# State-space powers from a table of exponents on TensorE and ScalarE sines; phases of the chunk states on VectorE

## The reference

```
dt   = exp(log_dt);  A = -exp(A_re_log) + 1j * A_im;  dtA = A * dt
C    = (C_re + 1j * C_im) * expm1(dtA) / A
K    = 2 * einsum('hn,hnl->hl', C, exp(dtA[:, :, None] * l)).real      # l = 0 .. L-1
y    = causal_convolution(z, K) + z * D_skip                           # z = layernorm(h)
y    = gelu(y);  out = W @ y + b;  h = h + out[:H] * sigmoid(out[H:])   # four such layers
```

## Time and profile before

| | |
|---|---|
| median of 3 executions | 1387.14 us (1383.18 to 1394.52) |
| profiled execution, own time | 1394.2 us |
| its span (first to last instruction) | 1392.4 us |
| mean granted TensorE clock | 0.817 of full |
| busy: PE, DVE, ACT, POOL | 939.7, 936.1, 482.8, 508.0 us |
| state-space stage (four layers and prologue) | 0 to about 464 us of the span |

### The profile page before, as it was taken

How to read it: one execution, slowest core, us unless ns; L and a number is a source line. 1 busy time by engine, 2 the same in 40 slices (tenths; PEclk the granted TensorE clock), 3 DMA queues, 4 the chain that set the end, 5 groups by cost and what they waited for, 6 DMA issues and landing times.

```text
span 1392.4 us, 19437 instructions
## 1 busy us (share of the span) xinstructions
PE 939.7 (67%) x7176; PEld 625.3 (45%) x7176; DVE 936.1 (67%) x1586; ACT 482.8 (35%) x1204; POOL 508.0 (36%) x384
## 2 busy tenths in 40 slices
PE   4052262262273617999999967759889788979877
PEld 4032042141042306787878743324466443546543
DVE  5999899799785663464645468968855346955443
ACT  3133043043031422121212141016677334768622
POOL 4862832832710360000000032437934133954310
PEclk9575685685685758999999978979989779979968
DMA  1151071071071418454544040000011200012100
GB/s 59 40 92 32 3 130 32 2 129 30 0 129 30 183 44 146 91 91 90 90 90 90 0 147 0 0 0 0 16 46 49 80 24 25 1 31 62 32 0 30
DMA packets 60445, 75.52 MB, mean 54 GB/s; under 512 B 37544, under 2 KB 42036, under 8 KB 58676
## 3 DMA queue, kind: packets, MB, share of 16 engines
q1 hardware_dynamic: 60376, 74.60, 24.5%
HBM read 52.11 MB, written 1.51 MB: 39 GB/s over the span
## 4 chain that ended last, share of the span: by engine, by line
PE 39%; DVE 29%; POOL 13%; issue 10%; ACT 5%; DMA 2%; SPq 0%; DVEq 0%; POOLq 0%; ACTq 0%
PE bank L960 6%; PE bank L962 6%; PE bank L961 6%; POOL rest L1190 3%; ACT rest L1143 3%; POOL rest L1180 3%; PE bank L1378 2%; POOL rest L1186 2%; PE bank L641 2%; DVE kept L379 2%; DVE main L534 2%; PE bank L1387 2%; DVE rest L453 2%; PE bank L1445 2%; PE bank L1446 2%
## 5 line engine op out<-in xcount | busy, mean ns | idle before, releaser
L406 POOL TENSOR_TENSOR kept<-kept 128x8 f32<-128x8 f32 x20 | 4.0, 201 | 456.9 <-DVE kept L383 456.9
L1143 ACT ACTIVATE rest<-bank,main 128x128 f32<-128x128 f32 x256 | 113.4, 479 | 12.4 <-POOL main L1201 10.8
L641 PE MATMUL bank<-main,rest 128*128 128x512 f32 x64 | 38.6, 759 | 92.3 <-DVE main L573 86.5
L807 ACT ACTIVATE x_high<-main 128x512 fp32r<-128x512 f32 x48 | 30.3, 633 | 199.1 <-DVE main L881 199.1
L960 PE MATMUL bank<-x_high,w_low 128*128 128x512 f32 x192 | 76.7, 399 | 20.4 <-DVE x_low L886 20.4
L629 PE MATMUL bank<-main 128*32 128x64 f32 x1024 | 22.4, 270 | 99.2 <-DMA main<-main 98.8
L1209 POOL TENSOR_TENSOR rest<-rest,main 128x512 f32<-128x512 f32 x64 | 65.4, 1043 | 47.3 <-DVE main L1274 47.3
L420 ACT ACTIVATE main<-bank,kept 128x128 f32<-128x128 f32 x40 | 14.5, 469 | 185.7 <-POOL kept L413 185.7
L881 DVE TENSOR_TENSOR main<-kept,rest 128x512 f32<-128x512 f32 x48 | 33.0, 690 | 68.1 <-PE bank L962 43.7
L961 PE MATMUL bank<-x_low,w_high 128*128 128x512 f32 x192 | 76.2, 397 | 0.0
L960 PE MATMUL bank<-hid_high,w_low 128*128 128x512 f32 x192 | 75.6, 394 | 0.7 <-DVE main L905 0.7
(11 more groups left out here) (283 smaller groups left out, 2873.1 us busy)
## 6 DMA issues: line engine op xcount, KB each, us to landing
rest<-share_d SPq DMA_DIRECT2D x4, 3072.0 KB, 21.4
rest<-share_d SPq DMA_DIRECT2D x4, 2304.0 KB, 20.3
main<-main SPq DMA_DIRECT2D x32, 256.0 KB, 5.1
main<-k_pad SPq DMA_DIRECT2D x16, 512.0 KB, 7.4
rest<-main SPq DMA_DIRECT2D x32, 256.0 KB, 3.4
main<-w_dram SPq DMA_DIRECT2D x2, 3072.0 KB, 14.5
main<-main SPq DMA_DIRECT2D x32, 128.0 KB, 2.3
rest<-tables_dram SPq DMA_DIRECT2D x2, 2048.0 KB, 9.2
```

The lines of the kernel that those rows point to most:

```text
L641: last = T.matmul(bank[4 + 2 * (b % 2) + k][:, :], w_out[:, k * P:(k + 1) * P], rhs, start=True, stop=True)
L1143: last = A.activation(probs[:, p, 4 * r + m, :], bank[2 * p + r][:, m * P:(m + 1) * P], ACT.Exp, scale=row_scale[:, c, r, m:m + 1], bias=r ...
```

## The change

- The angles and exponents no longer come from broadcast products of GpSimd and VectorE. `dta` (rate and angle per turn, 64 columns) is transposed on TensorE, copied by ScalarE to `dtaT`, and multiplied with a table `expo` (64 rows of 3072 floats, block-diagonal, loaded once: 768 KB) in PSUM: 4 products of 512 columns for the near angles, 2 for the far ones, 4 for the magnitudes' exponents. All have 32 rows of contraction.
- ScalarE adds `MAGIC` to round to whole turns (`s4_act_round_near`, `_far`), VectorE subtracts in one instruction each (`s4_dve_near_turns`, 2048 wide, `s4_dve_far_turns`, 1024 wide), in place of three parts and a clamp. ScalarE takes the sines at all 64 near powers directly (three passes of 2048) and exponentiates the magnitudes in PSUM (one pass of 2048).
- `pow_re`, `pow_im` are two VectorE instructions of 2048 with the magnitude read from PSUM. There are no anchors, `k_re`, `k_im`, and no GpSimd part.
- The coefficients go into the weights (`sel_re`, `sel_im`, 128x4 per channel) and the kernel rows come from 64 products of 64 columns (each with weights of its own), laid on four partition groups; ScalarE copies them with 4 + 4 copies, and SyncE writes them with 4 DMAs instead of 1.
- `g_re`, `g_im` (the phases times the coefficient) move from GpSimd to the end of `s4_dve_powers`, six VectorE instructions of 1024. GpSimd keeps `decay`, which waits for the layer's `s4_u_re`.
- The prologue makes layer 0's angles ahead of `LN_A` on VectorE. The loops over layers are written out; marker increments (`turn`) are gone; some semaphores of later stages are merged.

The diff, cut to its core:

```diff
-        def s4_dve_angles(dve, G):
...
-            V.tensor_tensor(mag, dta[:, 0, :].unsqueeze(2).to_broadcast([P, HG, NEAR]),
-                            expo[:, 0:NEAR].unsqueeze(1).to_broadcast([P, HG, NEAR]), ALU.mult).then_inc(sem("s4_marg"), 1)
-        def s4_dve_reduce(dve, chain, G):
...
-            for part in (TWO_PI_1, TWO_PI_2, TWO_PI_3):
-                link(V.scalar_tensor_tensor(theta, turns, -part, theta, ALU.mult, ALU.add))
-            V.tensor_scalar(theta, theta, 3.1415925, -3.1415925, ALU.min, ALU.max).then_inc(sem("s4_theta"), 1)
+        def s4_dve_near_turns(dve, G):
+            dve.wait_ge(sem("s4_rounded"), G * 2 + 1)
+            nc.vector.scalar_tensor_tensor(turns, turns, MAGIC, near(HIGH_BANKS), ALU.subtract, ALU.subtract).then_inc(sem("s4_turns"), 1)
...
+        def s4_dve_powers(dve, chain, G, mag):
+            V.tensor_copy(s0, pow_re[:, :, FIRST])
+            link(V.tensor_copy(mag1, mag[:, :, FIRST]))
+            V.tensor_tensor(pow_im, pow_im, mag, ALU.mult).then_inc(sem("s4_pow_im"), 1)
+            V.scalar_tensor_tensor(pow_re, pow_re, 1.0, mag, ALU.subtract, ALU.mult, reverse0=True).then_inc(sem("s4_pow_re"), 1)
...
-            V.tensor_tensor(four(pow_re), hi(anc_re), lo(anc_re), ALU.mult)
-            link(V.tensor_tensor(four(k_re), hi(anc_im), lo(anc_im), ALU.mult))
-            V.tensor_tensor(pow_re, pow_re, k_re, ALU.subtract).then_inc(sem("s4_pow_re"), 1)
-            dve.wait_ge(sem("s4_pow_re"), G + 1)
-
-            V.tensor_tensor(k_re, pow_re, c2_re.unsqueeze(2).to_broadcast([P, HG, CHUNK]), ALU.mult).then_inc(sem("s4_k_re"), 1)
+            V.tensor_tensor(sel_re, sel[:, 0, :].unsqueeze(1).to_broadcast(wide), c2_re.unsqueeze(2).to_broadcast(wide), ALU.mult)
+            V.tensor_tensor(sel_im, sel[:, 1, :].unsqueeze(1).to_broadcast(wide), c2_im.unsqueeze(2).to_broadcast(wide), ALU.mult).then_inc(sem("s4_sel"), 1)
...
+            V.tensor_tensor(gr, phi_c, c2r, ALU.mult)
+            V.tensor_tensor(gi, phi_c, c2i, ALU.mult)
+            V.tensor_tensor(g_x, phi_s, c2i, ALU.mult)
+            link(V.tensor_tensor(g_y, phi_s, c2r, ALU.mult))
+            V.tensor_tensor(gr, gr, g_x, ALU.subtract)
+            V.tensor_tensor(gi, gi, g_y, ALU.add).then_inc(sem("s4_phases"), 1)
...
+        def s4_pe_near_angles(pe, G):
+            pe.wait_ge(sem("s4_dtaT"), G + 1)
+            for k in range(4):
+                last = nc.tensor.matmul(bank[4 + k][:, :], dtaT[HG:2 * HG], expo[HG:2 * HG, 512 * k:512 * k + 512], start=True, stop=True)
+            last.then_inc(sem("s4_x_ps"), 1)
...
+            pe.wait_ge(sem("s4_sel"), L + 1)
+            for hh in range(HG):
+                q, at = hh // PIECE, CHUNK * (hh % PIECE)
+                dst = bank[4][32 * q:32 * q + GROUPS, at:at + CHUNK]
+                T.matmul(dst, sel_re[:, hh, :], pow_re[:, hh, :], start=True, stop=False)
+                last = T.matmul(dst, sel_im[:, hh, :], pow_im[:, hh, :], start=False, stop=True)
+            last.then_inc(sem("s4_k_ps"), 1)
...
             pe.wait_ge(sem("s4_back"), (L + 1) * (HG // 2))
-            pe.sem_inc(sem("turn"), 1)
+            if more:
+                s4_pe_near_angles(pe, L + 1)
             pe.wait_ge(sem("s4_z"), L + 1)
...
+            if more:
+                s4_pe_far_angles(pe, L + 1)
+                pe.wait_ge(sem("s4_in"), L + 1)
+                s4_pe_exponents(pe, L + 1, 0)
...
+        def s4_act_sines_near(act, G):
+            act.wait_ge(sem("s4_turns"), G * 2 + 1)
+            if G:
+                act.wait_ge(sem("s4_pow_moved"), G * 128)
+            A.activation(pow_im, turns, ACT.Sin, scale=-TURN)
+            A.activation(pow_re, turns, ACT.Sin, scale=-TURN / 2).then_inc(sem("s4_sin"), 1)
+            act.wait_ge(sem("s4_sin"), G * 2 + 1)
+            A.activation(pow_re, pow_re, ACT.Square, scale=math.sqrt(2.0)).then_inc(sem("s4_sin"), 1)
...
             if more:
-
-                act.wait_ge(sem("s4_phases"), L + 1)
-                s4_act_decay(act, L + 1)
-            if more:
-                s4_act_sines(act, L + 1, CLOSE, "s4_sin")
-
+                s4_act_round_near(act, L + 1)
+                s4_act_sines_near(act, L + 1)
+                s4_act_round_far(act, L + 1)
+                s4_act_sines_far(act, L + 1)
+                s4_act_magnitudes(act, L + 1, LOW_BANKS)
             act.wait_ge(sem("s4_u"), L + 1)
-            if more:
-                s4_act_sines(act, L + 1, FAR, "s4_sin_far")
...
+        def s4_pool_phases(pool, chain, G):
+            pool.wait_ge(sem("s4_mag"), G * 2 + 1)
+            if G:
+                pool.wait_ge(sem("s4_u_re"), G)
+            G_.tensor_tensor(decay[:, :, 1:CHUNKS], r_chunk[G % 2].unsqueeze(2).to_broadcast([P, HG, CHUNKS - 1]),
+                             ones.unsqueeze(1).to_broadcast([P, HG, CHUNKS - 1]), ALU.mult).then_inc(sem("s4_decay"), 1)
```

More of the change, by code:

```diff
@@ L81, in exponents @@
 def exponents():
-    e = [LOW - 1 - b for b in range(LOW)] + [LOW * (HIGH - 1 - a) for a in range(HIGH)] + [CHUNK * c for c in range(CHUNKS)]
-    return np.array(e, np.float32)
+    near, far = CHUNK - 1 - np.arange(CHUNK), CHUNK * np.arange(CHUNKS)
+    rows = [np.kron(np.eye(HG), e) for e in (near, far)]
+    return np.tile(np.concatenate(rows, axis=1), (2, 1)).astype(np.float32).reshape(-1)
 class Chain:
@@ new lines, in s4_pe_far_angles, with s4_pe_exponents @@
+        def s4_pe_far_angles(pe, G):
+            pe.wait_ge(sem("s4_turns"), G * 2 + 1)
+            for k in range(2):
+                at = NEAR_COLS + 512 * k
+                last = nc.tensor.matmul(bank[4 + k][:, :], dtaT[HG:2 * HG], expo[HG:2 * HG, at:at + 512], start=True, stop=True)
+            last.then_inc(sem("s4_x_ps"), 1)
+        def s4_pe_exponents(pe, G, first):
+            for k in range(4):
+                last = nc.tensor.matmul(bank[first + k][:, :], dtaT[0:HG], expo[0:HG, 512 * k:512 * k + 512], start=True, stop=True)
+            last.then_inc(sem("s4_x_ps"), 1)
@@ new lines, in s4_act_rates, with s4_act_dtaT, s4_act_round_near @@
+            A.activation(r_chunk[G % 2], dta[:, 0, :], ACT.Exp, scale=float(CHUNK)).then_inc(sem("s4_mag"), 1)
+        def s4_act_dtaT(act, G):
+            act.wait_ge(sem("s4_dtaT_ps"), G + 1)
+            nc.scalar.activation(dtaT, bank[6][0:2 * HG, 0:P], ACT.Copy).then_inc(sem("s4_dtaT"), 1)
+        def s4_act_round_near(act, G):
+            act.wait_ge(sem("s4_x_ps"), G * 3 + 1)
+            if G >= 1:
+                act.wait_ge(sem("s4_phases"), G)
+            nc.scalar.activation(turns, near(HIGH_BANKS), ACT.Copy, bias=MAGIC).then_inc(sem("s4_rounded"), 1)
@@ L725, in s4_pool_angles @@
-        def s4_pool_angles(pool, chain, G):
-            G_ = nc.gpsimd
-            wide = [P, HG, N_EXP]
-            def link(instruction):
-                chain.link(instruction)
-                pool.sem_inc(sem("turn"), 1)
-            pool.wait_ge(sem("s4_dta"), G + 1)
-            link(G_.tensor_tensor(theta, dta[:, 1, :].unsqueeze(2).to_broadcast(wide),
-                                  expo.unsqueeze(1).to_broadcast(wide), ALU.mult))
-            link(G_.tensor_scalar(turns, theta, 1.0 / (2 * math.pi), MAGIC, ALU.mult, ALU.add))
-            G_.tensor_scalar(turns, turns, MAGIC, None, ALU.subtract).then_inc(sem("s4_turns"), 1)
```

358 lines of the change are left out of this document (169 added, 189 removed).

## The result

The changed kernel takes **1336.8 us** (median of 4 executions, 1330.3 to 1343.5) against 1386.3 for the kernel before (4 executions): a ratio of 0.963, interval 0.957 to 0.970. It is faster by 50 us, and the forecast of 1320 had expected 67.5. The profiled execution took 1339.3, its span is 1337.5.

The account below looks back on a forecast made before the run. VectorE, held up by GpSimd's work, was taken to bound the state-space layers. Savings of 28.4 (prologue, layer 0), 35.6 (two middle layers) and 3.5 (layer 3) sum to 67.5: 1387.1 becomes 1319.6, said as 1320, range 1304 to 1350.

Parts of the forecast that it names:

- rival D: VectorE's holds come from something other than GpSimd and stay: minus 20 instead of minus 67, 1367 us; chance 0.04.
- rival C: Weight load and product do not overlap in the kernel rows, 0.22 us a record: +80, so 1400 us; chance 0.05.
- the wait: VectorE idle in a middle layer from the norm's end at 20.0 to ScalarE's rounding of near angles at 25.3.
- The chain: TensorE and ScalarE work before the near turns: kernel rows, copies, near angles, rounding; done 25.3 us into a middle layer.
- rival A: The new TensorE and ScalarE chain is off the path, VectorE alone sets the time: 1312 us; chance 0.14.
- the pace of the state products: State products behind the near angles in middle layers run at 2.4 GHz: 3.6 us instead of 7.05.
- Rival B: TensorE at 1.2 GHz from kernel rows through state products: +11 each middle layer, 1359 us; chance 0.10 with half-way cases.
- the lower end of the range: Fastest total time the forecast allowed: 1304 us, with the new chain off the path and a lighter prologue.
- The 6.9 us for the kernel rows: Lower estimate for a layer's 128 kernel-row records, by columns from L641 at 0.054 each; the forecast took 7.5.
- The term costed at nothing: Written-out layer loops and markers costed at 0, since layer 0 was written out already and its L619 took no longer.
- Layer 0: Prologue and first layer: prologue powers end at 68.9, the layer at 149.9 against 178.3, minus 28.4 us.
- The second half of the change: The six phase instructions moved from GpSimd to VectorE's powers, costed at 6.9 us of the 17.3 us powers.

Follow-up runs that it names:

- e9: Changed kernel with the kernel-row products and ScalarE's copies of layers 1 to 3 moved into the layer before: 1331.9 us, 0.957 of the kernel before.
- e2: Changed kernel with each layer's Toeplitz transfer issued only after its state products: 1335.9 us, 0.958 of the kernel before.
- e7: Changed kernel with angle and exponent products reading 64 rows instead of 32, the added rows zero: 1341.0 us in one execution.
- e6: Kernel before the change with only the six phase instructions moved from GpSimd to the end of VectorE's powers: 1406.4 us, ratio 1.011.
- e4: Changed kernel with the six phase instructions given back to GpSimd, behind decay: 1325.9 us, 0.951 of the kernel before.
- e3: Changed kernel with one unused product added behind each group of four back transposes: 1353.4 us, 0.973 of the kernel before.

## Why the prediction was right, and where it was not

**Right in kind.** The blocking went (rival D): L529 2.50 for four, small instructions 0.2, powers 16.7 against 17.3. Load and product overlap in the kernel rows (rival C): 0.056 a record, where 0.058 was taken and 0.19 would have turned the sign. The norm was done at 20.0, as forecast to a tenth; near angles at 22.8 (23.2), near turns at 27.0 (27.6), the wait at 4.72 and 5.41 (5.3). The chain is on the path, as e9 shows by taking it off, so rival A fell. The Trainium skill (TensorE: Matmul & The Clock Gate, Back-to-back issue gap) would have had 81 ns a record; by the 0.056 of this trace the rule does not hold for these products, whose weights are 4 columns wide.

**The step that failed** is the pace of the state products: "The pause before them falls away, so I take 2.4 GHz: 3.6 instead of 7.05". The pause ahead of them did fall away. The clock fell all the same, within or right behind the near angles, and with the stop inside them they take 8.5 us in layer 1. This moved the last transpose from 30.1 to 32.1 there, and to 33.0 in layer 2, where the transposes of the powers were slow too; the powers, 0.6 shorter, and small savings gave 1.1 of it back. The state products end 4.5 us later than forecast in layer 1 and only 2.0 of it shows, as the transposes wait for the near turns anyway. The small savings that gave part of it back were in no term of the forecast: luck. The forecast read the granted clock as a matter of gaps alone. The runs show that the rows of the products ahead matter: with 32 of the 128 the clock falls, with 64 it stays for the state products. Rival B named this clock, but began it at the kernel rows, which ran at 1.00; it was right for the state products alone.

Two slips in the working touch the lower end of the range only. The 6.9 us for the kernel rows "by columns alone" is not what L641's row gives: 3.70 us for eight records of 512 columns is 0.058 for 64, or 7.4 us. And rows between 6.9 and 18 move a layer by minus 0.6 to plus 10, not from minus 2.

**The term costed at nothing** is "The written-out loops and the markers I cost at 0". Layer 0 had been written out before and had no pause, but its program was shorter and its state products came at the pace of 1.2 GHz. With the written-out program the products of layer 3, which did run at 2.4 GHz, stop for 3.85, and with the clock lost in that pause they take 9.25 instead of 3.6. That is 5.7 of the 6.1 by which layer 3 missed. e2 takes back 3.4 of it.

**Layer 0** was 3.7 late. The prologue's powers end at 70.9 instead of 68.9, and the last transpose at 98.5 instead of 93.8: 2.0 from the prologue, 0.7 from near turns that come later still, 2.0 from the pace of the state products, and 1.0 is made good behind them. In the prologue TensorE's far angles and exponents, kernel after, ran at half pace from end to end, and VectorE waited for TensorE's next work behind them:

```profile
26.81 3.77 PE L604 MATMUL psum<-main 32*128 32x512 f32 x4 [4.37 <-DVE rest L444]
...
32.96 7.19 PE L610 MATMUL psum<-main 32*128 32x512 f32 x8 [2.37 <-DVE rest L450]
...
41.23 1.66 DVE L393 TENSOR_SCALAR kept<-psum,kept 128x512 f32<-128x512 f32 x2 [1.29 <-PE psum L366]
```

The forecast had some 2 us for the far angles and nothing on the path for the exponents. The half pace here is not a matter of 32 rows alone: e7 had it with 64.

**The second half of the change** was costed rightly, 6.9 on VectorE's path, and counted as part of a net gain. e6 and e4 show that it should have been judged by itself: once the powers need no GpSimd, GpSimd can make the phases during the transposition and the gate, where VectorE has nothing with two SBUF inputs to be held.

## What to carry to other kernels

When an engine held by another is freed, ask again for every job that was moved to get away from the hold: the phases were better left on GpSimd, in a stretch where VectorE only transposes or waits. Cost a stretch of small products by the clock that its neighbours leave, and look at how many rows the products ahead use, not only at gaps. Faster work that is fed by a written-out program can run into its own instruction supply: look for pauses marked "issue" with nothing that releases them, and at what the DMA queues moved in the microseconds before, ahead of counting a saving.

## What the runs showed of the hardware that was not expected

- The granted clock fell to 0.50 in a stretch where TensorE was 100% busy with 32-row products of 512 float32 columns. With 64 rows and the same columns it stayed at 1.00 through the near angles and 152 records and more behind them. Where it was low already, in the prologue, eight records took 7.19 us with 32 rows and with 64, while the kernel rows there (128 rows, 4 weight columns) brought it back to 1.00 5.4 us after their start. Which property of the products counts beside the rows was not tried. The granted clock as shown can't be trusted at the start of some programs: in e7 it reads 1.00 while eight records of 512 columns take 7.16 us; the pace tells.
- TensorE stopped for 0.7 to 4.7 us inside a run of identical products, behind the same record of 256 (167, 160, 152 and 154 in layers 0 to 3) in each kernel that stops (137 in layer 3 where layers 1 and 2 are a loop), in written-out layers and not in a loop (there, once, near the end of y's products). With products at half pace it happened only where a transfer of some 200 GB/s had run beside them, up to 2.8 us before the restart, and not where that had ended earlier (layer 0 of the kernel after, layer 2 of e4); with products at 2.4 GHz it happened without the transfer too.
- GpSimd's two-input instructions hold a VectorE instruction with two inputs in SBUF (L499, 128 elements: 1.99 instead of 0.29), but not a transpose (3.68 against 3.62) and not one whose second input lies in PSUM (L464: 2.28).
- One plain product behind each four transposes lengthened a group from 0.49 us, at which ScalarE's copies set the pace, to 0.82, with TensorE never idle (e3).
